# A decoder layer on one core: block-wise loads of the routing's row groups, halved loads of the second expert weights, and two more experts' weights loaded in the expert stage

## The reference

```python
x = x + attention(layernorm(x), w_q, w_kv, w_dense)        # causal, 16 heads of 128, 4 groups
x = x + xattn(layernorm(x), ctx, mask, mask, Wq, ...)      # 16 heads of 16 over 512 positions
x = x + moe(layernorm(x), Wg, W1, W2, W3, bias)            # 8 experts, top 2 of sigmoid scores

# moe, on T = 4096 tokens h of length 512:
p = sigmoid(h @ Wg.T)                      # 4096 x 8
top2 = top_k(p + bias, 2)
w = p[top2] / sum(p[top2])
out = sum over the two experts e of  w_e * (silu(h @ W1[e].T) * (h @ W3[e].T)) @ W2[e].T
```

## Time and profile before

| | |
|---|---|
| Median of 3 runs | 2860.67 us (2858.1 to 2871.18) |
| The profiled execution | 2866.61 us, of which the span is 2864.8 us |
| TensorE matmul / weight load | 91% / 63% of the span |
| VectorE / ScalarE / GpSimd | 66% / 51% / 35% |
| Mean granted TensorE clock | 0.966 of full speed |
| DMA | 290.70 MB, mean 101 GB/s |

### The profile page before, as it was taken

One profiled execution on the slowest core, in us unless ns is written; L12 is line 12 of the kernel. 1 busy time (PEld: TensorE's weight loads), 2 busy tenths in 40 slices (PEclk: granted clock), 3 DMA queues, 4 the chain that ended last, 5 costly groups with the idle time before them and its releaser, 6 DMA issues. The chain is left out here.

```text
span 2864.8 us, 50062 instructions
## 1 busy us (share of the span) xinstructions
PE 2602.2 (91%) x14768; PEld 1801.6 (63%) x14769; DVE 1885.6 (66%) x3845; ACT 1455.5 (51%) x2868; POOL 996.1 (35%) x1178
## 2 busy tenths in 40 slices
PE   7999999999999999999489999898999876399997
PEld 6888888888788888888333333333333322277776
DVE  6556655555655444555488888888888877576765
ACT  4334433334433333344157767776777665355554
POOL 1112221111211111122426556555665546433332
PEclk9999999999999999999689999999999998699998
DMA  3201222202211011110657777777777777755554
GB/s 147 74 15 58 73 73 73 73 31 102 89 59 54 35 59 44 44 59 30 123 92 127 136 138 139 125 134 141 139 129 133 139 153 254 260 102 104 110 107 85
DMA packets 141571, 290.70 MB, mean 101 GB/s; under 512 B 39600, under 2 KB 42544, under 8 KB 135872
## 3 DMA queue, kind: packets, MB, share of 16 engines
q1 hardware_dynamic: 113184, 223.38, 33.3%
q0 software_dynamic: 23664, 58.09, 9.6%
q10 hardware_dynamic: 4656, 8.40, 1.0%
HBM read 147.82 MB, written 81.68 MB: 80 GB/s over the span
## 5 line engine op out<-in xcount | busy, mean ns | idle before, releaser
L1577 DVE TENSOR_REDUCE b_negmax<-b_ps_s 128x2 f32<-128x1024 f32 x512 | 615.5, 1220 | 105.8 <-PE b_ps_s L1762 100.2
L1376 ACT ACTIVATE b_probs<-b_ps_s 128x1024 f32<-128x1024 f32 x512 | 517.2, 1020 | 229.0 <-PE b_ps_s L1773 226.4
L278 POOL TENSOR_SCALAR probs<-probs,rinv 128x256 f32<-128x256 f32 x256 | 242.0, 945 | 1094.1 <-DVE rinv L435 1094.1
L312 ACT ACTIVATE probs<-ps_s,negmax 128x128 f32<-128x128 f32 x256 | 94.1, 368 | 485.0 <-DVE negmax L428 485.0
L1762 PE MATMUL b_ps_s<-b_stack 54*128 54x512 f32 x1024 | 231.4, 449 | 92.0 <-ACT b_probs L1376 42.9
L1773 PEld LDWEIGHTS b_ps_s<-b_stack 56*128 56x128 f32 x1024 | 97.2, 186 | 309.2 <-issue 195.7
L1784 PE MATMUL b_ps_o<-b_probs,b_v_stack 128*32 128x512 f32 x2048 | 281.5, 622 | 1.5 <-ACT b_probs L1376 1.1
L1773 PE MATMUL b_ps_s<-b_stack 56*128 56x512 f32 x1024 | 254.9, 494 | 27.8 <-ACT b_probs L1376 14.4
L543 PE MATMUL ps_proj<-xT_h,wq_h 128*128 128x512 f32 x512 | 215.7, 421 | 0.0
L2467 POOL DMA_INDIRECT out<-e_y,e_place_int x71 | 118.8, 1674 | 250.9 <-DMA out<-e_y,e_place_int 210.6
L543 PE MATMUL ps_proj<-xT_h,wq_l 128*128 128x512 f32 x512 | 201.7, 394 | 0.0
(11 more groups left out here) (334 smaller groups left out, 6628.6 us busy)
## 6 DMA issues: line engine op xcount, KB each, us to landing
b_stack<-b_split SPq DMA_DIRECT2D x240, 128.0 KB
e_row<-rows_by_expert SPq DMA_DIRECT2D x71, 258.0 KB, 2.9
b_out_tiles<-row_sum_inverses SPq DMA_DIRECT2D x64, 256.0 KB
x<-acc SPq DMA_DIRECT2D x15, 1024.0 KB, 5.0
b_stack<-b_late SPq DMA_DIRECT2D x96, 128.0 KB
x_in<-in_x SPq DMA_DIRECT2D x8, 1024.0 KB, 8.3
normalised_x_split<-xT_h SPq DMA_DIRECT2D x8, 1024.0 KB, 10.0
normalised_x_split<-xT_l SPq DMA_DIRECT2D x8, 1024.0 KB, 11.1
```

The costliest lines, as they stand in the source:

```text
L278: nc.gpsimd.tensor_scalar(probs[:, s, P:3 * P], probs[:, s, P:3 * P], rinv[:, s, 1:2], None, ALU.mult).then_inc(probs_done, 1)
L312: nc.scalar.activation(probs[:, s, 0:P], ps_s[s][:, 0:P], ACT.Exp, bias=negmax[:, s, 0:1], accum_out=rowsum[:, s, 0:1])
L1376: nc.scalar.activation(probs[:, k % 2, p, :, :], ps[:], ACT.Exp, scale=0.25).then_inc(e_done, 1)
L1577: nc.vector.tensor_reduce(negmax[:, k, p, :], ps[:], AX.X, ALU.max, negate=True).then_inc(m_reduced, 1)
```

## The change

Four things are changed.

1. The rows of a group are loaded as four DMAs of 128 rows (256 KB) instead of one of 512 rows (1024 KB). Each adds 16 to the group's semaphore, so that a complete group is now 64 (128 on second use).
2. The blocks are issued one per turn. Group 0 in two pairs on SP; group 1 in the four turns of quad 3 of the last sequence but one; groups 2 to 5 in the turns of quads 0 to 3 of the last sequence: `route_load(2 + q, k)`. Before, groups 2, 3, 4 and 5 were issued whole in turns (0,1), (0,3), (1,2) and (2,0). Groups 6 and 7 stay where they were, as four DMAs in a row.
3. The second weights of experts 4 to 7 are loaded directly behind group 7, those of experts 0 to 3 where all of them were loaded before. The expert stage waits for both.
4. The first weights of experts 4 and 5 are no longer loaded in the routing. ScalarE loads them at the start of the expert stage, and those of experts 6 and 7 in tiles 1 and 2. The splits of experts 4 to 7 come one tile later on both engines.

```diff
                     if tail and not last:
                         sp.wait_ge(y_stored, 16 * HQ * 12)
-                        route_load(0)
+                        route_load(0, (0, 1))
                         route_small()
...
                     stack_negmax(b, 2)
+                    if tail and not last:
+                        route_load(0, (2, 3))
                     if not last:
                         wait_alone(sp, tile_low, 4 * (b + 2), (consts, 4))
...
                 route_load(7)
-                for e in range(2, 6):
+                route_load_down(4, 8)
+                for e in range(2, 4):
                     route_weights(e)
                 route_finish()
...
-                        if tail and not last and (q, k) == (3, 0):
-                            act.wait_ge(raw_done, len(TILES) * B)
-                            act.wait_ge(vbias_done, len(VALUES) * B)
-                            act.wait_ge(tile_low, len(TILES) * B)
-                            act.wait_ge(y_stored, 16 * HQ * 12)
-                            route_load(1)
+                        if tail and not last and q == 3:
+                            if k == 0:
+                                act.wait_ge(raw_done, len(TILES) * B)
+                                act.wait_ge(vbias_done, len(VALUES) * B)
+                                act.wait_ge(tile_low, len(TILES) * B)
+                                act.wait_ge(y_stored, 16 * HQ * 12)
+                            route_load(1, k)
...
-                    for G, turn in ((2, (0, 1, 1)), (3, (0, 3, 1)), (4, (1, 2, 1)), (5, (2, 0, 0))):
-                        if at == turn:
-                            if G == 5:
-                                for quad in range(QUADS - 1):
-                                    act.wait_ge(stacked[quad], STACKS[quad] * B)
-                                act.wait_ge(half_stacked, HALF_STACKS * B)
-                                act.wait_ge(late_copied, 16 * B)
-                            route_load(G)
+                    if p:
+                        if at == (3, 0, 1):
+                            for quad in range(QUADS - 1):
+                                act.wait_ge(stacked[quad], STACKS[quad] * B)
+                            act.wait_ge(half_stacked, HALF_STACKS * B)
+                            act.wait_ge(late_copied, 16 * B)
+                        route_load(2 + q, k)
...
-    LOADED = {**{G: (x2_loaded[G], 16) for G in range(6)}, 6: (x2_loaded[0], 32), 7: (x2_loaded[3], 32)}
+    LOADED = {**{G: (x2_loaded[G], 64) for G in range(6)}, 6: (x2_loaded[0], 128), 7: (x2_loaded[3], 128)}
...
-            sp.dma_start(group_rows(G)[:, :, 0:H], x2_rows[G].rearrange("(n p) h -> p n h", p=P)).then_inc(LOADED[G][0], 16)
+            for n in blocks:
+                sp.dma_start(group_rows(G)[:, n, 0:H], x2_rows[G][n * P:(n + 1) * P, :]).then_inc(LOADED[G][0], 16)
...
             sp.wait_ge(logits_out, GROUPS)
-            sp.dma_start(w2[:], w_2T.rearrange("e (k p) h -> p e k h", p=P)).then_inc(w2_loaded, 16)
+            load_down(0, E // 2)
...
+        def load_down(first, last):
+            sp.dma_start(w2[:, first:last], w_2T[first:last].rearrange("e (k p) h -> p e k h", p=P)).then_inc(w2_loaded, 16)
...
-        RAW_FIRST, SPLIT_FIRST = 6, 4
+        RAW_FIRST, SPLIT_FIRST = 4, 4
...
-                    if isinstance(u, int) and SPLIT_FIRST <= u + 4 < E:
-                        weights_high(u + 4)
+                    if isinstance(u, int) and SPLIT_FIRST <= u + 3 < E:
+                        weights_high(u + 3)
+                    if isinstance(u, int) and RAW_FIRST + 2 <= u + 5 < E:
+                        load_weights(u + 5)
...
-                act.wait_ge(w2_loaded, 16)
+                act.wait_ge(w2_loaded, 32)
...
-                for e in range(RAW_FIRST, E):
+                for e in range(RAW_FIRST, RAW_FIRST + 2):
                     load_weights(e)
...
-                    if isinstance(u, int) and SPLIT_FIRST <= u + 3 < E:
-                        weights_low(u + 3)
+                    if isinstance(u, int) and SPLIT_FIRST <= u + 2 < E:
+                        weights_low(u + 2)
```

More of the change, by code:

```diff
@@ L2040, in sync_parts, with load @@
     def sync_parts(sp):
-        def load(G):
+        def load(G, blocks=range(TB)):
             if G == 6:
                 sp.wait_ge(scattered[SLOTS[G]], 16 * 2 * TB)
-            sp.dma_start(group_rows(G)[:, :, 0:H], x2_rows[G].rearrange("(n p) h -> p n h", p=P)).then_inc(LOADED[G][0], 16)
+            for n in blocks:
+                sp.dma_start(group_rows(G)[:, n, 0:H], x2_rows[G][n * P:(n + 1) * P, :]).then_inc(LOADED[G][0], 16)
         def load_small():
@@ L2072, in finish @@
             sp.wait_ge(w13_loaded[1], 16 * (RAW_FIRST - RAW_APART))
-        return load, load_small, load_weights, finish
+        def load_down(first, last):
+            sp.dma_start(w2[:, first:last], w_2T[first:last].rearrange("e (k p) h -> p e k h", p=P)).then_inc(w2_loaded, 16)
+        return load, load_small, load_weights, load_down, finish
     def gpsimd_parts(pool):
@@ L2156, in finish, with load @@
                 act.dma_start(rows[bass.ds(r, P), :], pad_rows[:]).then_inc(padded[1], 16)
[L2158 to L2159 removed]
+        def load(G, n):
+            act.dma_start(group_rows(G)[:, n, 0:H], x2_rows[G][n * P:(n + 1) * P, :]).then_inc(LOADED[G][0], 16)
         return load, apply, copy, copy_logits, exponentials, weights_high, finish
```

4 lines of the change are left out of this document (1 added, 3 removed).

## The result

| | before | after |
|---|---|---|
| Median | 2868.01 us (20 runs, 2855.68 to 2875.88) | 2873.74 us (20 runs) |
| Ratio to the kernel before | | 1.0026, 95% interval 1.0014 to 1.0038 |
| Profiled execution | 2866.61 us, span 2864.8 us | 2873.74 us, span 2872.3 us |
| Mean granted TensorE clock | 0.966 | 0.963 |

One execution among the 20 of the changed kernel (9708 us) and one of the twelve of experiment 4 (3277 us) were disturbed and are left out of the ratios. The ratio is 7.5 us on 2868 us (the medians differ by 5.7): slower beyond its interval, but by less than the half per cent that counted as a difference in the forecast. The forecast was +3.3 us. It was given against a median of 2860.67 us from three runs; with 20 the kernel before has 2868, so its absolute number, 2864, lies some 10 us too low, 7 of them from that base.

The account below looks back on a forecast made before the run. The prediction took GpSimd's row of scatters, started by VectorE's placing of group 1, to bound the routing's tail. Its terms -1.0 - 1.5 + 0.5 + 6.0 + 0.3 - 2.5 + 1.5 gave +3.3 us, 2864 us; range 2850 to 2876.

Parts of the forecast that it names:

- Group 5 goes late: Routing: group 5's last block leaves with the last exponential, so group 1 is placed later; +6.0 us, bounds +5.0 to +9.7.
- Group 1 in four blocks: Cross attention: spreading group 1's load shortens TensorE's stall only a little; -1.0 us, between 0 and -6.1.
- the comparison of rates: Group 1's load: blocks ask for 84 KB/us, the single transfer got 76, so the spread load is as heavy.
- the stall of group 1 vanishes: Rival, cross attention: TensorE's stall at group 1's load goes, 5.1 us more gained, 2859 us; chance 0.15.
- Group 2 in blocks: Cross attention: fewer bytes lie ahead of the row sums at group 2's load; -1.5 us, between 0 and -2.8.
- Group 0's second half: Cross attention: it stands on SP's queue just ahead of stacks TensorE waits for; +0.5 us, between 0 and +2.
- four issues for groups 6 and 7: Routing, SP: three more issues of about 0.4 us, GpSimd feels at most one; +0.3 us, between 0 and +1.
- The tail: Routing's end: 2 MB less under way, so the last scatters land sooner; -2.5 us, between 0 and -3.0.
- Experts: Expert stage: weight splits come one tile later, a free tile becomes a costly one; +1.5 us, 0 to +1.6.
- The slower rival: Routing: the second weights' upper half crowds out scatters, over 1.27 us from one to the next; +8.9 us, 2870; chance 0.2.
- The chain to the end: Routing's tail: GpSimd's 64 scatters nearly end to end set its end, starting when VectorE has placed group 1, 2387.8 us.
- Long scatters are contention with VectorE's subtractions: Routing's tail: the 2.75 us scatter lies on VectorE's 2.28 us subtraction, not a full queue; nothing of it is won.

Follow-up runs that it names:

- experiment 4: Kernel before with only group 1 loaded as four blocks, one per turn of quad 3; 2867.44 us, ratio 0.9987 to the kernel before.
- experiment 9: Kernel before with only group 5 loaded late, as four blocks in the turns of the last quad; 2871.08 against 2862.39 us, ratio 1.0031.
- experiment 3: Changed kernel with group 5's blocks issued beside group 4's and the second weights' upper half behind experts 2 and 3's first weights; 2868.40 us, ratio 1.0002.
- experiment 5: Changed kernel with only the block-wise loads left, group 5's in quad 2, second weights and experts as before; 2868.86 us, ratio 0.9998 to the kernel before.
- experiment 10: experiment 6 with the experts' first weights held back until group 6's logits are made; 2865.76 us, ratio 1.0010 to the kernel before.
- experiment 11: experiment 10 with the first weights of experts 0 and 1 let go directly behind group 7; 2870.53 us, ratio 0.9992 to the kernel before.
- experiment 2: Changed kernel with the second weights' upper half issued behind the first weights of experts 2 and 3; 2872.19 us, ratio 1.0012 to the kernel before.
- experiment 6: experiment 5 with group 7 loaded ahead of the first weights of experts 0 and 1; 2866.73 us, ratio 0.9991 to the kernel before.

## Why the prediction was right, and where it was not

The time was right: +3.3 us forecast, +7.5 measured, inside the range and within half a per cent. That the term of the late group would outweigh the gains was right too. Several other steps were not. They cancelled, and that the sum came out so near is in part luck.

- **Group 5 goes late, +6.0 us: right in place, and the term that decides.** The block issued with the last exponential was waited for 15.96 us (some 12 forecast), GpSimd's second group of scatters starts 11.95 us behind that exponential (2391.30 against 2379.35; some 13 forecast). The cost in time is clear of noise only in experiment 9, +8.9 us; the other two comparisons give 3 to 4 us, within their intervals. One piece was missing. TensorE comes out of the wait at half clock, and the next logits take 5.89 us instead of 3.59. That is 2.3 of the 3.5 us by which the loss grows from group 1's places (3.2 us) to group 2's (6.7 us); VectorE's wait for TensorE's products there adds most of the rest (1.40 us instead of 0.26). I had moved the chain rigidly and not asked what an idle TensorE does afterwards.
- **Group 1 in four blocks, -1.0 us: wrong mechanism, size open.** The step that failed is the comparison of rates, 84 against 76 KB/us. TensorE's two waits do not sum to 5 to 7 us but to 0.5. The rival "the stall of group 1 vanishes" had this right and was wrong in what followed. First, the stall of 7.24 us is only partly the kernel's: its larger wait is absent from the second profile of before. The 27th exponential is 65.4 us behind the common event in the mean of the four profiles with one transfer for group 1, and 61.6 in the nine with all groups in blocks: 3.8 us. Group 1 alone (experiment 4) has 65.1. Second, at the last exponential 2.2 us of it are left (81.2 and 79.0 in the same means), not clear of noise, since the single profiles there run from 76.7 to 85.0 and from 75.3 to 83.4. The runs of experiments 3 and 5 (1.0002, 0.9998) show nothing of it.
- **Group 2 in blocks, -1.5 us:** the wait for the row sums fell by 1.86 us (2.23 to 0.37), but a new one of 2.15 us came, VectorE's for group 1's last block. It is part of the 2.2 us above.
- **Group 0's second half, +0.5, and four issues for groups 6 and 7, +0.3:** nothing to be seen; the wait at 2282.70 is even 0.43 us shorter.
- **The tail, -2.5 us: wrong, at most 1.0 and nothing is shown.** The last scatter to the first tile takes 11.2 us in the changed kernel, against 12.2 in the first profile of before and 11.2 in the second. With no weights held back, all profiles that pause have 11.2, with part 4 and without; the two that don't have 12.2 and 12.5 (before, experiment 9), and none with part 4 is of that kind. The failed step is the assumption that the landing of the last scatters answers to 2 MB less. It answers to more traffic behind the last scatters: with weights held back until the end the stretch grows to 13.7 and 13.0 us in experiments 10 and 11.
- **Experts, +1.5 us: right,** 1.3 us.
- **The slower rival, second weights crowd out the scatters: refuted in its mechanism.** The scatters of groups 3 and 4 stand at 1.27 us as before, and experiment 2 moved the half away without shortening a wait. What did wait in that stretch, group 7's rows, stood behind other weights.
- **The chain to the end, GpSimd's row of scatters: incomplete.** Its row carries the end from group 5 on, but in the changed kernel its start there is set by VectorE's places of group 5 (a wait of 3.96 us), and these by ScalarE's copies of group 6, which I had taken as hidden. In the first profile of before, where the copies take 2.4 us, GpSimd does not wait for these places.
- **Long scatters are contention with VectorE's subtractions: borne out.** In the changed kernel the places in the program have moved and the pairs with them: scatters of 2.86 and 2.77 us lie on subtractions that start at 2444.63 and 2453.01, while all scatters between 2416.75 and 2437 take 0.96 to 1.09 us in fuller DMA engines (a share of 1.02, and 0.86 in 2445 to 2456). It agrees with the Trainium skill (GPSIMD Engine Reference, Key points), which has GpSimd share SBUF interfaces with VectorE.

No version is shown to beat the kernel before. The lowest ratios are those of experiments 4 (0.9987), 6 (0.9991) and 11 (0.9992), all with 1 in their interval.

## What to carry to other kernels

Before a term of a sum is taken from a single profiled execution, see whether it is the kernel's: here a stall of 3.8 us, a wait of 2 us and a stretch at full clock were all missing from a second profile of the same code, and the spread of the runs (5 us) was as large as the sum. Splitting and spreading a load took away a stall of its neighbours here, of which nothing is shown in the time, but its last block sets when its reader can start: put it where the reader has slack, not in the last turn (here 8.9 us, experiment 9). When a wait is taken away and the time stays, look for the next one beneath it (here group 7's rows, then ScalarE's copies, then the weights themselves). And before an edit is credited with what a profile no longer shows, look ahead of the place where the edit acts: if the profile differs there already, the edit may not be the cause.

## What was not expected of the hardware

- **A pausing ScalarE.** With the 16 DMA engines full (a share of 1.00 to 1.04), five ScalarE instructions that take 2.45 us without pauses took 12 to 18 us in eleven of fourteen profiles; the last of them started 10.3 us behind its input in the changed kernel (2435.33, the input made at 2425.03). In the same eleven ScalarE had started its 30th exponential 1.27 to 2.42 us late, 39 us or more before. The three profiles without the one were without the other, two of them with full engines at the copies (1.04) and one with engines at 0.60 (experiment 10). The cause is open.
- **A load's landing is set by its queue.** 1 MB behind 2 MB in SP's queue reached its reader in 14.5 to 19.1 us, ahead of them in 8.2 to 8.4 us, at the same total traffic. Whether it was issued as one transfer or four made no difference (18.9 and 19.0 us, experiments 4 and 3).
- **Half clock behind a wait.** After 6.57 us without work TensorE ran at 1.2 GHz and returned to 2.4 within the next logits (5.89 us instead of 3.59, mean granted clock 0.61). These logits were slow in all three kernels with a late group and in no other. The logits of group 1, which lie ahead of that wait, took 4.02 to 6.54 us in the profiles of different kernels, and 4.88 and 5.93 us in two executions of the kernel before.
